# Low and up product of the blocked inverse interleaved head by head on four 64x64 quadrants

## What is computed

```python
def step(S, inp):
    q_t, k_t, v_t, g_t, b_t = inp
    Sk = jnp.einsum('bhkv,bhk->bhv', S, k_t)
    delta = jnp.einsum('bhv,bhk->bhkv', v_t, k_t) - jnp.einsum('bhv,bhk->bhkv', Sk, k_t)
    S = jnp.exp(g_t)[..., None, None] * S + b_t[..., None, None] * delta
    o_t = jnp.einsum('bhkv,bhk->bhv', S, q_t)
    return (S, o_t)
```

## Time and profile before

| what | value |
|---|---|
| median of 3 runs | 5441.39 us (5434.37 to 5447.08) |
| the profiled execution: its own time, its span | 5438.13 us, 5436.4 us |
| granted TensorE clock over the span | 0.954 |
| TensorE busy (matmul) | 4902.0 us, 90% |
| VectorE, ScalarE, GpSimd busy | 3220.0, 2100.8, 1163.5 us |
| matmul records | 62913 |
| instruction queue (q8) | 504 packets, 8.26 MB |

### The profile page before, as it was taken

One profiled execution on the slowest core, in us unless ns is written; L12 is line 12 of the kernel. 1 busy time (PEld: TensorE's weight loads), 2 busy tenths in 40 slices (PEclk: granted clock), 3 DMA queues, 4 the chain that ended last, 5 costly groups with the idle time before them and its releaser, 6 DMA issues. The chain is left out here.

```text
span 5436.4 us, 154184 instructions
## 1 busy us (share of the span) xinstructions
PE 4902.0 (90%) x62913; PEld 2767.9 (51%) x62913; DVE 3220.0 (59%) x5633; ACT 2100.8 (39%) x2965; POOL 1163.5 (21%) x1361
## 2 busy tenths in 40 slices
PE   6877869999999999999766679999999999999998
PEld 5333369999999999876444422222222222222222
DVE  4889944444444444433344457767777777777766
ACT  1666622222222222213322225555555555555554
POOL 1444533233232332310144440000000000000000
PEclk9999989999999999999877769999999999999999
DMA  2322231111111111122322230000000000000000
GB/s 98 125 93 93 93 108 49 51 56 46 57 48 51 50 49 59 48 62 77 113 61 61 61 81 7 7 11 8 11 8 11 8 11 8 11 8 11 8 11 8
DMA packets 201321, 249.55 MB, mean 46 GB/s; under 512 B 52864, under 2 KB 132864, under 8 KB 199968
## 3 DMA queue, kind: packets, MB, share of 16 engines
q1 hardware_dynamic: 180240, 209.29, 12.3%
q0 software_dynamic: 6144, 16.79, 1.0%
q10 hardware_dynamic: 14352, 14.55, 0.8%
HBM read 135.18 MB, written 105.38 MB: 44 GB/s over the span
## 5 line engine op out<-in xcount | busy, mean ns | idle before, releaser
L2078 DVE TENSOR_REDUCE part_max<-p_m 128x1 f32<-128x512 f32 x2112 | 1363.8, 687 | 639.7 <-PE p_m L1933 634.7
L2060 ACT ACTIVATE prob<-p_s 128x1024 f32<-128x1024 f32 x1024 | 1047.9, 1024 | 1035.6 <-PE p_s L1989 1034.2
L1951 PE MATMUL p_o<-prob,v_one 128*64 128x512 f32 x4096 | 1105.0, 618 | 0.7 <-ACT prob L2060 0.7
L1933 PE MATMUL p_m<-keys,queries 96*128 96x512 f16 x2112 | 694.3, 388 | 46.2 <-DMA keys<-parts_d 19.6
L1989 PE MATMUL p_s<-queries,keys 97*128 97x512 f16 x2048 | 618.5, 383 | 1.2 <-ACT queries L2043 1.2
L1989 PEld LDWEIGHTS p_s<-queries,keys 97*128 97x128 f16 x2048 | 136.7, 97 | 654.9 <-ACT prob L2060 534.0
L1933 PEld LDWEIGHTS p_m<-keys,queries 96*128 96x128 f16 x2112 | 206.6, 98 | 512.0 <-DVE part_max L2078 290.1
L544 PE MATMUL p_proj<-xn_t_all,proj_w_sb 128*128 (+1 forms) x768 | 390.9, 652 | 78.4 <-ACT raw L570 70.4
L1904 POOL TENSOR_TENSOR attn<-o_num,o_inv 32x512 f32<-32x512 f32 x64 | 80.8, 1262 | 1601.2 <-DVE o_inv L2097 1594.7
L1050 DVE TENSOR_TENSOR inv<-inv,pd_pre 128x512 f32<-128x512 f32 x256 | 176.2, 688 | 406.2 <-PE pd_pre L795 406.2
L962 ACT ACTIVATE inv_low<-pd_low 128x512 f32<-128x512 f32 x320 | 191.1, 597 | 575.7 <-PE pd_low L833 525.5
(11 more groups left out here) (240 smaller groups left out, 6643.1 us busy)
## 6 DMA issues: line engine op xcount, KB each, us to landing
k_d<-qkv SPq DMA_DIRECT2D x8, 2048.0 KB, 7.5
q_d<-qkv SPq DMA_DIRECT2D x8, 2048.0 KB, 12.3
v_d<-qkv SPq DMA_DIRECT2D x8, 2048.0 KB, 7.3
sums<-sums_d SPq DMA_DIRECT2D x128, 128.0 KB, 3.0
k_t<-k_d SPq DMA_DIRECT2D x64, 256.0 KB, 3.3
q_t<-q_d SPq DMA_DIRECT2D x64, 256.0 KB, 3.4
v_t<-v_d SPq DMA_DIRECT2D x64, 256.0 KB, 4.9
slots_d<-zero ACTq DMA_DIRECT2D x1, 10112.0 KB, 32.0
```

The source lines that it names most:

```text
L1933: te.matmul(p_m[k % 2][:], queries[0:ROW, p, hh, sub * P:(sub + 1) * P], keys[0:ROW, 2 * p + hh, kb * BLK:(kb + 1) * BLK], start=True, sto ...
L1951: product = te.matmul(p_o[64 * hh:64 * hh + VW, :], g.v_one[:, j, p, hh:hh + 2, :].rearrange("p a d -> p (a d)"), prob[:, j % 2, hh, :], s ...
L2060: a.activation(prob[:, j % 2], p_s[j % 2][:], ACT.Exp, scale=SCORE_SCALE).then_inc(exp_d, 1)
L2078: v.tensor_reduce(part_max[:, hh * SUB + sub, kb:kb + 1], p_m[k % 2][:], AX.X, ALU.max).then_inc(red_d, 1)
```

## The change

A second helper, `across(hs)`, gives the other half of the partitions. `low` and `up` of a level become one function `low_up`: for each head one matmul of the low product and one of the up product, 32 matmuls in turn. Both read their operands from the same half of the partitions; the up product goes to the same half of PSUM, the low product to the other. The two heads together so use all four quadrants. For this `inv` and `step` have their heads swapped between the halves: `half` and `residual` now write across, `updates` reads across and writes back. The 2x2 inverse must be swapped too: GpSimd makes it in `step`, `first_low` carries for each head a second matmul that moves it across into `p_pre` with the identity as weights, and ScalarE copies it from there into `inv` (`keep_moved`). The level 5 product (`last_up`) stays as it was.

```diff
-    half_d, step_d, lowmm_d, lowc_d, upmm_d, up_d = (sem2(s) for s in ("half", "step", "lowmm", "lowc", "upmm", "up"))
+    half_d, step_d, lowmm_d, lowc_d, upmm_d, up_d, moved_d, movedc_d = (
+        sem2(s) for s in ("half", "step", "lowmm", "lowc", "upmm", "up", "moved", "movedc"))
...
+    def across(hs):
+
+        return slice(C - hs.start, 2 * C - hs.start)
...
         def first_low(n, x):
-            wait_apart(pe, g, (att_d[x], n.now), (inv1_d[x], n.now))
+            wait_apart(pe, g, (att_d[x], n.now), (inv1_d[x], n.now), (rows_d[x], n.now))
             for p, hs in heads():
-                last = te.matmul(p_low[x][hs, p, :], inv[x][hs, p, :], g.c("eye_c")[hs, :], start=p == 0, stop=False, skip_group_check=True)
-            last.then_inc(lowmm_d[x], 1)
+                low_mm = te.matmul(p_low[x][hs, p, :], step[x][hs, p, :], g.c("eye_c")[hs, :], start=p == 0, stop=False, skip_group_check=True)
+                move = te.matmul(p_pre[x][across(hs), p, :], g.c("eye_c")[hs, :], step[x][hs, p, :], start=True, stop=True)
+            low_mm.then_inc(lowmm_d[x], 1)
+            move.then_inc(moved_d[x], 1)
 
         def half(n, x, k):
-            freed = (rows_d[x], n.now) if k == 1 else (up_d[x], n.level[k - 1])
+            freed = (movedc_d[x], n.now) if k == 1 else (up_d[x], n.level[k - 1])
             wait_apart(pe, g, freed, (lowc_d[x], n.level[k]))
-            each(p_pre[x], of(upper[x]), of(inv_low[x])).then_inc(half_d[x], 1)
-
-        def low(n, x, k):
+            for p, hs in heads():
+                last = te.matmul(p_pre[x][across(hs), p, :], upper[x][hs, p, :], inv_low[x][hs, p, :], start=True, stop=True)
+            last.then_inc(half_d[x], 1)
+
+        def low_up(n, x, k):
             wait_apart(pe, g, (step_d[x], n.level[k]))
             for p, hs in heads():
-                last = te.matmul(p_low[x][hs, p, :], inv[x][hs, p, :], step[x][hs, p, :], start=False, stop=k == NL - 1, skip_group_check=True)
-            last.then_inc(lowmm_d[x], 1)
-
-        def up(n, x, k):
-            if k == NL:
-                wait_apart(pe, g, (step_d[x], n.level[k]))
+                os = across(hs)
+                low_mm = te.matmul(p_low[x][hs, p, :], inv[x][os, p, :], step[x][os, p, :], start=False, stop=k == NL - 1, skip_group_check=True)
+                up_mm = te.matmul(p_pre[x][os, p, :], step[x][os, p, :], inv[x][os, p, :], start=True, stop=True)
+            low_mm.then_inc(lowmm_d[x], 1)
+            up_mm.then_inc(upmm_d[x], 1)
+
+        def last_up(n, x):
+            wait_apart(pe, g, (step_d[x], n.level[NL]))
             each(p_pre[x], of(step[x]), of(inv[x])).then_inc(upmm_d[x], 1)
 
...
-                te.matmul(p_a[hs, p, :], v_t[hs, r, p, :], g.c("eye_c")[hs, :], start=True, stop=False)
-                last = te.matmul(p_a[hs, p, :], k_g[hs, r, p, :], state[hs, p, :], start=False, stop=True)
+                te.matmul(p_a[across(hs), p, :], v_t[hs, r, p, :], g.c("eye_c")[hs, :], start=True, stop=False)
+                last = te.matmul(p_a[across(hs), p, :], k_g[hs, r, p, :], state[hs, p, :], start=False, stop=True)
...
-            each(p_b, of(inv_fin, n.ring[x]), of(resid)).then_inc(w_d, 1)
+            for p, hs in heads():
+                os = across(hs)
+                last = te.matmul(p_b[hs, p, :], inv_fin[os, n.ring[x], p, :], resid[os, p, :], start=True, stop=True)
+            last.then_inc(w_d, 1)
...
                     for x in range(2):
-                        low(pre, x, k)
-                        up(pre, x, k)
+                        low_up(pre, x, k)
                     half(pre, 0, k + 1)
```

On the other engines:

```diff
+        def keep_moved(n, x):
+            act.wait_ge(up_d[x], n.level[0])
+            act.wait_ge(moved_d[x], n.now)
+            a.activation(inv[x][:], p_pre[x][:], ACT.Copy).then_inc(movedc_d[x], 1)
...
-                keep_low(pre, 0, 0)
-                keep_low(pre, 1, 0)
+                for x in range(2):
+                    keep_low(pre, x, 0)
+                    keep_moved(pre, x)
...
         def add_up(n, x, k):
             if k == 1:
-                dve.wait_ge(inv1_d[x], n.now)
+                dve.wait_ge(movedc_d[x], n.now)
...
-            po.tensor_tensor(inv[x][:], upper[x][:], over_pairs(g.c("couples")), ALU.mult).then_inc(off_d[x], 1)
+            po.tensor_tensor(step[x][:], upper[x][:], over_pairs(g.c("couples")), ALU.mult).then_inc(off_d[x], 1)
             pool.wait_ge(off_d[x], n.now)
-            po.tensor_tensor(inv[x][:], over_pairs(g.c("eye_c")), inv[x][:], ALU.subtract).then_inc(inv1_d[x], 1)
+            po.tensor_tensor(step[x][:], over_pairs(g.c("eye_c")), step[x][:], ALU.subtract).then_inc(inv1_d[x], 1)
```

More of the change, by code:

```diff
@@ L913, in one @@
             if pre is not None:
-                up(pre, 0, NL)
+                last_up(pre, 0)
             if post is not None:
@@ L917, in one @@
             if pre is not None:
-                up(pre, 1, NL)
+                last_up(pre, 1)
         couples(pe, one)
```

## The result

The changed kernel takes 5462.66 us (median of 5 runs, 5461.45 to 5469.66); the kernel before on the same chip took 5441.39 (5 runs, 5434.37 to 5447.23). The ratio is 1.0041, interval 1.0026 to 1.0055: slower, by 21 us, where +50 was forecast. Run again in two later sets of runs it was 1.0060 [1.0047, 1.0074] and 1.0048 [1.0035, 1.0061].

The account below looks back on a forecast made before the run. The loop was taken as bound by instruction fetch more than by TensorE's array. An added block, +4.0, less 0.9 gained made +3.1 us a trip, +50 us over 16 trips' worth: 5490 us, range 5445 to 5540.

Parts of the forecast that it names:

- The bound: In the delta loop, TensorE waits for instruction blocks: the array wants 3.73 us each, five fetched blocks averaged 4.09 us.
- a round at best: Shortest time from entering one instruction block to being able to enter the next in the loop: 3.54 us.
- The rule of the Trainium skill: Rival: instruction fetch keeps up, so low and up products give back 239 us, 5200 us in all; chance 0.08.
- What it adds: In the loop, first_low's extra matmuls fill one more instruction block a trip, costing 4.0 us.
- The moved copy of ScalarE: At level 1, half of chunk 1 waits about 0.55 us for ScalarE's second copy; costed at nothing, covered by a stop.
- What it removes: At levels 1 to 4, low and up overlap on four quadrants; array time falls 7.5 us a couple, 0.9 a trip gained.
- the first rival: Low and up on four quadrants do not overlap; 77 us slower, 5515 us; chance 0.16.
- The step that failed: Gain from low and up's shorter array time in the loop: 0.9 us a trip, bounds 0 and 2.7.
- a drain as the upper bound: Changing diagonal at half, residual and updates drains the array: 2.2 us a couple at most, taken as nothing.
- The two terms of the sum: For each loop trip: +4.0 us for the added instruction block and -0.9 us for the shorter array.
- The clock: Rival: idle TensorE drops to 1.2 GHz in the loop, over 200 us more if for half of it; 0.06 together with drains.

Follow-up runs that it names:

- copy_again: Second measurement of the changed kernel with ScalarE copying both halves of step into inv instead of TensorE matmuls moving the inverse: 5427.15 us, 0.9927 of the kernel before.
- copying kernel: The changed kernel with ScalarE copying both halves of step into inv, without matmuls that move the inverse: 0.9938 and 0.9927 of the kernel before in two sets.

## Why the prediction was right in sign and too large

*The bound* held. TensorE stands at block ends, a trip has 26 transfers as forecast, and they come no closer than before: the two closest starts of q8 in the loop are 3.27 us apart before and 3.33 after, and the mean fell from 4.17 to 4.05. (The 3.54 that the prediction called a round at best was too long by that.) A trip takes 105.4 us, where 107 was forecast. Of the 153 us of array time that left the loop a quarter came back at best (40 us, copy_again). The rule of the Trainium skill (Runtime: NRT & Kernel Launch, Instruction fetch mechanics) that the fetch is hidden would have given a gain of 239 us; no run here gained more than 40.

*What it adds*: a round of 4.0 us a trip was forecast for the move, 64 us in all; taking the move out of the changed kernel gave 61 to 67. The moved copy of ScalarE did as said. In order of time on ScalarE, at level 1:

```profile
2005.44 0.60 ACT L980 ACTIVATE inv_low<-pd_low 128x512 f32<-128x512 f32 x1 [1.91 <-PE pd_low L827]
2005.94 0.59 ACT L976 ACTIVATE inv<-pd_pre 128x512 f32<-128x512 f32 x1
```

and `half` of chunk 1 on TensorE behind it:

```profile
2006.63 0.76 PE L836 MATMUL pd_pre<-inv_low,upper 64*64 64x64 f32 x19 [0.28 <-issue]
```

It starts 0.10 us behind the end of the copy (2005.94 + 0.59), after 0.28 us idle. What that is worth alone was not tried.

*What it removes*: four quadrants do overlap, 15 ns a record, as forecast, so the first rival falls. Their credit was put at 0.9 us a trip, 14 us; on the copying kernel head by head is 9 to 14 us faster than one product after the other. That is the order alone, with both products on the quadrants of the change.

**The step that failed** is the term of -0.9 us a trip, all that a shorter array was to give back. The prediction held the loop to be bound by the fetch more than by the array: the array wants 3.73 us a block, the fetch gives one in 4.09, so only a third of 14 blocks could gain, 0.19 us each; and the other diagonal of `half`, `residual` and `updates` was put at nothing, with a drain as the upper bound. The change without its move, at 25 transfers a trip as before, is 33 and 40 us faster than before: the shorter array gives back 2.1 to 2.5 us a trip. With the +4.0 of the move that makes +1.5 to +1.9 a trip, +24 to +30 us; measured were +22, +33 and +26 (by the ratios). I had looked for what a change of diagonal could cost and not for what it could give, though the overlap of heads on different quadrants was in the argument already.

The earlier trace rows could have warned: TensorE is busy for 1402.0 us in 350 blocks, 4.01 us each and not 3.73, which is the time of a block of nothing but small products of two quadrants. On average the array stood close to the 4.09 that I took for the fetch's.

*Where the missing credit lies* is shown for the copying kernel only: there, `residual` and `updates` put back cost 24 us, 1.5 a trip, and the interleaving is worth 9 to 14. In the changed kernel itself the same diagonals are worth about 5 us, not told from nothing. `half` on the other diagonal was never put back.

The two terms of the sum don't stand alone, and the same miss can be put on the other one. The block added to the kernel before costs 34 us, 2.1 a trip and not 4.0; with it in place the shorter array gives back 7 us by the ratios, less than the 14 forecast. What fails in both orders is the assumption behind both terms, that the 25 transfers alone set the time of the kernel before. It was 33 to 40 us longer than the same transfers allow with a shorter array. An added block takes up part of this room where it is there, and costs a full round where the shorter array has used it up.

*The clock* was a rival, with the sentence that nothing in the loop shows it falling. It fell a little. Windows of 1 us of the changed kernel (length, then PE, PEld, DVE, ACT, POOL busy and records, the clock, the DMA share, GB/s):

```profile
2026.80:2027.80 1.00, 0.07 (x3) 0.00 (x0) 0.44 (x1) 0.23 (x1) 0.00 (x0) 1.00 1.00 369
2027.80:2028.80 1.00, 0.00 (x0) 0.00 (x0) 0.00 (x0) 0.00 (x0) 0.00 (x0) 1.00 0.73 261
2028.80:2029.80 1.00, 0.94 (x29) 0.95 (x31) 0.00 (x0) 0.00 (x0) 0.00 (x0) 0.73 0.20 72
2029.80:2030.80 1.00, 1.00 (x30) 1.00 (x23) 0.68 (x1) 0.00 (x0) 0.00 (x0) 0.50 0.09 24
...
2032.80:2033.80 1.00, 1.00 (x70) 0.95 (x65) 0.69 (x1) 0.01 (x1) 0.00 (x0) 1.00 0.07 16
```

The loads of the next chunks fill the DMA engines (share 1.00), TensorE stands for 2 us, and then runs at 1.2 GHz for some 3.4 us. The clock records of the loop have 82 us at this level (76 and 92 in the other two traces of the changed kernel, 44 and 55 in those of the copying kernel, none in the kernel before). Products on two quadrants start 53 ns a record there and 29 at 2.4 GHz, so of 82 us at most 45%, 37 us, was lost, and of the copying kernel's at most 20 to 25. Some of it is not felt, as TensorE waits for the next block anyhow; how much was not isolated. In the copying kernel's two traces, of the first 13 trips each, the ten trips with the clock at 2.4 GHz throughout took 102.4 us and the seven with more than 6 us at 1.2 GHz 105.1; but a slow fetch both lengthens a trip and makes the stop ahead of the fall, so this is not the clock's price alone. The clock is thus an open part of all comparisons between a short and a long array, and may be part of why the block costs more in the changed kernel than in the kernel before.

## What to carry to other kernels

Where TensorE stops in the middle of a product with no semaphore to wait for, count its instructions and the transfers of the instruction queue: then fewer instructions may be worth more than a shorter array (here a copy by ScalarE in place of 16 small matmuls a chunk, 0.6 to 0.7% under the kernel before, turned a loss into a gain: the block had cost 61 to 67 us, and the shorter array gave back 33 to 40). Before an added block is priced, split the loop's blocks into those that the fetch paces and those that the array paces; their mean says neither. When a product moves to other quadrants of the array, ask which neighbours it can now overlap, and not only what the move may cost; but expect less than the overlap times the number of changes. Two terms that a sum adds may share the same waiting time, so price each with the other in place and without it.

## What was not expected of the hardware

- A small matmul starts before earlier ones on other quadrants have ended: a product of 32 records on the other diagonal starts 0.72 to 0.76 us behind the start of the one ahead, 0.93 on the same. The Trainium skill (TensorEngine Tiling (Array Packing), Key Properties) says that tiles operate independently and that only a change of the tiling mode drains; this trace agrees with the first. Of the second the trace before has a case in each output projection, whose tiles are 128x64: its first matmul starts 0.15 us behind the start of the last matmul of a 64x64 product (median of 56), where starts inside that product are 0.03 apart.
- What a loop costs depends on where it begins within a block of 256 instructions: 128 instructions ahead of it made 26 transfers a trip of 25 and cost 12 us, 256 left 25 and cost 4 us.
- A stop of 2 us in a dense stretch was followed by some 3.4 us at 1.2 GHz; not every such stop was.
- The kernel before took 5441 to 5467 us (medians) in the five sets of runs, more than most differences here; only ratios within a set told them apart.
